# An earlier gather of softmax sums, and two attention stages written out without their loop

## The reference

```python
def _attn(x, ctx, wq, wk, wv, wo, bo, heads):
    q = (x @ wq).reshape(b, n, heads, dh).transpose(0, 2, 1, 3)      # dh = 8, heads = 20
    k = (ctx @ wk).reshape(b, j, heads, dh).transpose(0, 2, 1, 3)
    v = (ctx @ wv).reshape(b, j, heads, dh).transpose(0, 2, 1, 3)
    a = softmax(einsum('bhid,bhjd->bhij', q, k) * dh ** -0.5)
    out = einsum('bhij,bhjd->bhid', a, v)
    return out.transpose(0, 2, 1, 3).reshape(b, n, heads * dh) @ wo + bo
h1 = _ln(x, n1_g, n1_b); x = _attn(h1, h1, ...) + x
h2 = _ln(x, n2_g, n2_b); x = _attn(h2, context, ...) + x
```

## Time and profile before

| | us |
|---|---|
| median of three runs | 4166.11 |
| lowest and highest run | 4163.22, 4181.46 |
| the profiled execution's own time | 4149.92 |
| its span, from first to last instruction | 4148.1 |

### The profile page before, as it was taken

How to read it: one execution, slowest core, us unless ns; L and a number is a source line. 1 busy time by engine, 2 the same in 40 slices (tenths; PEclk the granted TensorE clock), 3 DMA queues, 4 the chain that set the end, 5 groups by cost and what they waited for, 6 DMA issues and landing times. The chain is left out here.

```text
span 4148.1 us, 103517 instructions
## 1 busy us (share of the span) xinstructions
PE 3903.9 (94%) x38592; PEld 3363.6 (81%) x38592; DVE 2324.7 (56%) x4208; ACT 2173.5 (52%) x5452; POOL 1215.8 (29%) x1313
## 2 busy tenths in 40 slices
PE   5989879999998988999999999969999999999899
PEld 3766657777777987898888888858888888888799
DVE  3666634444434555666666666645556565555554
ACT  3665635555543445555555555535555555555344
POOL 4112111111104433333333333322222222232443
PEclk7888955555558999999999999989999999999999
DMA  3322212122111000000000000000000000000000
GB/s 99 90 75 71 76 46 69 47 57 56 53 37 30 0 19 23 1 0 0 0 0 0 0 0 0 1 23 3 2 2 2 2 2 2 2 2 1 16 19 21
DMA packets 97848, 98.23 MB, mean 24 GB/s; under 512 B 27664, under 2 KB 73104, under 8 KB 97680
## 3 DMA queue, kind: packets, MB, share of 16 engines
q1 hardware_dynamic: 94480, 94.50, 8.4%
q10 hardware_dynamic: 3200, 1.31, 0.1%
HBM read 20.76 MB, written 5.24 MB: 6 GB/s over the span
## 5 line engine op out<-in xcount | busy, mean ns | idle before, releaser
L1075 POOL TENSOR_TENSOR a_probs<-a_probs,a_rsums 128x1024 f32<-128x1024 f32 x160 | 303.7, 1898 | 750.4 <-DVE a_rsums L1173 750.4
L1095 ACT ACTIVATE a_probs<-a_scores_banks,a_negmax 128x128 f32<-128x128 f32 x1280 | 367.3, 377 | 297.4 <-DVE a_negmax L1161 297.4
L1075 POOL TENSOR_TENSOR c_probs<-c_probs,c_rsums 128x616 f32<-128x616 f32 x160 | 201.5, 1259 | 768.6 <-DVE c_rsums L1173 768.5
L1095 ACT ACTIVATE c_probs<-c_scores_banks,c_negmax 128x77 f32<-128x77 f32 x1280 | 313.2, 335 | 204.5 <-DVE c_negmax L1161 204.5
L1154 DVE COPY c_outT<-c_out_bank 128x512 f32<-128x512 f32 x160 | 110.7, 692 | 369.6 <-PE c_out_bank L1315 309.2
L1438 ACT ACTIVATE f_gate<-f_up_bank,bias 128x256 f32<-128x256 f32 x320 | 151.2, 473 | 286.4 <-PE f_up_bank L323 286.4
L1462 DVE SCALAR_TENSOR_TENSOR f_hidden<-f_up_bank,bias,f_gate 128x256 f32<-128x256 f32 x320 | 149.6, 481 | 254.3 <-ACT f_gate L1438 136.2
L1154 DVE COPY a_outT<-a_out_bank 128x512 f32<-128x512 f32 x160 | 110.7, 692 | 298.6 <-PE a_out_bank L1315 246.6
L686 ACT ACTIVATE c_probs<-c_scoresT_banks 77x1024 f32<-77x1024 f32 x160 | 163.1, 1019 | 175.3 <-PE c_scoresT_banks L805 175.2
L1161 DVE TENSOR_REDUCE a_negmax<-a_scores_banks 128x4 f32<-128x512 f32 x320 | 206.2, 686 | 73.8 <-PE a_scores_banks L1216 73.8
L743 DVE TENSOR_REDUCE a_negmax<-a_scores_banks 128x8 f32<-128x1024 f32 x160 | 194.8, 1218 | 90.3 <-PE a_scores_banks L788 89.1
(11 more groups left out here) (340 smaller groups left out, 11912.9 us busy)
## 6 DMA issues: line engine op xcount, KB each, us to landing
a_q_stack<-a_q_compact SPq DMA_DIRECT2D x96, 160.0 KB
a_k_stack<-a_k_compact SPq DMA_DIRECT2D x96, 160.0 KB
c_q_stack<-c_q_compact SPq DMA_DIRECT2D x96, 160.0 KB, 3.1
c_k_stack<-c_k_compact SPq DMA_DIRECT2D x96, 96.2 KB, 2.8
x_tokens<-in_x SPq DMA_DIRECT2D x16, 320.0 KB, 5.3
a_out<-a_heads SPq DMA_DIRECT2D x64, 80.0 KB, 2.6
c_out<-c_heads SPq DMA_DIRECT2D x64, 80.0 KB, 2.0
out_x<-x_tokens SPq DMA_DIRECT2D x32, 160.0 KB, 1.9
```

The costliest lines, as they stand in the source:

```text
L1075: nc.gpsimd.tensor_tensor(probs[i][:], probs[i][:], rsums[(k - 1) % 2][:].unsqueeze(2).broadcast_to([P, UNIT, NK]), ALU.mult).then_inc(s_p ...
L1095: done = nc.scalar.activation(probs[i][:, h, :], scores[:, h // GROUP, h % GROUP * NK:(h % GROUP + 1) * NK], ACT.Exp, bias=negmax[k % 2][: ...
```

## The change

Three edits, all in `attention_small`, so both `a0` and `c0` get them. First, `run` has no loop: quads 4 to 13 are written out as straight code like the others, and every wait there compares against a constant. Second, SP issues the gather of the sums ahead of the six stack DMAs of half 1, not behind them. Third, DVE takes the reciprocal at step 9, not at step 8.

```diff
         def run(engine, step, prepare=lambda k: None):
 
-            for k in range(-2 * QUNITS, 4 * QUNITS):
+            for k in range(-2 * QUNITS, (QUADS + 2) * QUNITS):
                 step(0, k)
                 if k < 0:
                     prepare(k + 2 * QUNITS)
-            with engine.Fori(2, QUADS // 2 - 1) as q:
-                for k in range(2 * QUNITS):
-                    step(q, k)
-            for k in range(4 * QUNITS):
-                step(QUADS // 2 - 1, k)
...
+                if s == 6 and live(prev, QUADS):
+                    sp.wait_ge(s_heads, GROUPS * (prev + 1))
+                    sp.dma_start(sums[:], heads[(local - 1) % 2][1:P:32, :, :]).then_inc(s_sums_in, 16)
                 if s in (5, 6) and live(nxt, QUADS):
                     half, par = s - 5, (local + 1) % 2
...
-                if s == 6 and live(prev, QUADS):
-                    sp.wait_ge(s_heads, GROUPS * (prev + 1))
-                    sp.dma_start(sums[:], heads[(local - 1) % 2][1:P:32, :, :]).then_inc(s_sums_in, 16)
...
-                if s == 8 and live(quad_of(q, k) - 1, QUADS):
+                if s == 9 and live(quad_of(q, k) - 1, QUADS):
                     dve.wait_ge(s_sums_in, 16 * quad_of(q, k))
                     nc.vector.reciprocal(sums[:], sums[:]).then_inc(s_rsums, 1)
```

## The result

The changed kernel takes 4063.35 us in the median of 4 runs (4055.39 to 4069.51). The kernel before took 4164.66 beside it (4159.23 to 4181.46). The ratio is 0.9744, with a 95% interval of 0.9716 to 0.9772. (The plain quotient of the two medians is 0.9757, which would give 4064.9, just inside; it lies in the interval too.) Either way the kernel is faster by 20 us or more than the 4086 that were forecast. The profiled execution went from 4149.9 to 4059.68 us, by 90.2.

A forecast was written before the change was run, and what follows sets the result against it. It took `a0` as bound by a PE pause each quad and the slow clock behind it, `c0` by PE at half clock. -72.7 - 4 + 0 = -76.7 us gave 4089 on the median, forecast 4086, range 4060 to 4128.

The forecast's parts named there:

- the pauses and the clock: In `a0`, removing PE's pause each quad also removes the slow clock behind it: 72.7 us, branch stops included.
- the end of `a0`: The quad from 528.90 us, slow throughout, gets partly faster: 4 us, bounds 0 and 8.5.
- The gather and the reciprocal: In `a0`, gather issued four us earlier behind six DMAs, reciprocal at step 9: DVE's 45.9 us wait goes.
- The pushed stacks and the `out` transfers: Half 1's stacks issue 0.61 us later, `out` as before; both still land in time, so costed at nothing.
- The twelve periods: Twelve quad periods of `a0` go from 380.8 to 308.0 us: 72.7 us gained.
- The clean quad: One `a0` quad between pauses at clock 1.00, 25.67 us, taken as what every quad would take.
- `c0`: Stage at 1.2 GHz with PE always busy: no change, 0 us, bounds -13 and +7.
- The loop's branch: In `a0`, PE's four stops for want of an instruction, 4.4 us, go with straight code; included in 72.7.
- Straight code in `c0` gives nothing: Writing out `c0`'s loop gains nothing: quads took 39.50 us before the loop and 39.41 inside it.
- The fetches: Rival: 27 further instruction fetches in `c0` each stop PE 1.1 us, 30 us more, 4116 us; chance 0.04.
- The 16 us of the median: Median runs 16 us above the profiled execution, place unknown; if part was slow clock in `a0`, it goes too.
- The rival of a settled slow clock: `a0` stays at the slow clock as `c0` does: 92 us more, 4258 us; chance 0.04.

The follow-up runs named there:

- e3: Changed kernel with the reciprocal back at step 8 (straight code and early gather kept): 4061.3 us, ratio 0.9779 to the kernel before.
- e7: Changed kernel with the loop back on DVE, ACT, POOL and SP in both stages, only PE straight: 4065.7 us, ratio 0.9747 to the kernel before.
- e8: Changed kernel with the loop back on PE alone in both stages, other engines straight: 4110.7 us, ratio 0.987 to the kernel before.
- e1: Changed kernel with the hardware loops back on all engines, gather and reciprocal still moved: 4109.1 us, ratio 0.9905 to the kernel before.
- e6: Changed kernel with the hardware loop back in `c0` alone, `a0` straight: 4078.8 us, ratio 0.9782 to the kernel before.
- e10: Changed kernel with the four projection tiles of each `c0` quad computed twice: 3956.8 us, ratio 0.9509 to the kernel before.
- e9: Changed kernel with `c0` projection tiles computed twice and `c0` scores widened from 78 to 128 columns: 3925.9 us, ratio 0.9428 to the kernel before.
- e2: Changed kernel with gather and reciprocal back in their old places, straight code kept: 4143.0 us, ratio 0.9963 to the kernel before.

## Why the prediction was wrong

The mechanism of the pauses and the clock was right and the sum too small: 76.7 us forecast in the profiled execution, 90.2 measured. The step that failed is the end of `a0`, costed at 4 us because "the clock may fall anyway"; it did not fall there, and the part measured 13.6. A smaller part of the miss is chance: 6.3 us are a stretch of fast clock in `c0`.

- **The gather and the reciprocal.** As forecast: issued behind six DMAs, and no wait of DVE. The pushed stacks and the `out` transfers cost nothing; PE waits 0.5 us for maxima and DVE never for the DMAs of `out` between 145 and 450 us. That the reciprocal had to be moved too was assumed, and e3 shows that it did not.
- **The twelve periods.** 76.8 us measured, 72.7 forecast. Both contain a thirteenth pause, which the prediction took for part of a period: from restart to restart PE's twelve periods are 378.2 us, not 380.8. The clean quad was taken as 25.67 us and is 25.33 in the mean of twelve (304.00/12). The quad it was read from was still in the loop: the loops of the other engines were forecast at nothing and cost 0.2 us a quad (e7 against the changed kernel), PE's own loop nothing in a quad without a branch (e8, 25.4 us). The rest of the 0.34 is in part the last of the twelve, which takes 24.6 us.
- **The end of `a0`**, and the part ahead of the periods. Forecast 4 us, bounds 0 and 8.5; measured 11.3 + 2.3. This is the term that failed most. The quad of 29.5 us at 0.50 was expected to stay slow in part, since PE is less packed in it. In the changed kernel the clock stayed at 1.00 all through it, and it takes 21.9 us from reciprocal to reciprocal (457.61 to 479.51), where it took 31.6 with its pause: nearly the whole of the upper bound came. The last interval behind it, which the forecast left out, went from 24.3 to 20.6 us, in part because the reciprocal stands a step later.
- **`c0`.** Forecast 0, bounds -13 and +7; measured -9.5. 6.3 of it are one more stretch of fast clock (a first quad of 32.7 us, not 39.0), which is luck in the sense of the prediction: it allowed for it and could not foresee it. 3.1 are the later reciprocal and no gain. So the 0 was right: e3, with one such stretch and the reciprocal at step 8, has 559.2 us beside 558.6.
- **The loop's branch.** The step "4.4 us at the loop's branch; straight code has none of them" put the wrong price on the wrong rows. The 4.4 us were the second stop of each branch turn. The first, 2.4 to 3.2 us, lay under the DMA pause and showed as a wait for maxima. The price of the four branches with their slow clock is about 36 us (e1). The sum was not hurt, since pause and branch went together and the clean quad had neither. A forecast for the moves alone, made with the same prices, would have been wrong: it would have given e1 almost all of the gain, and e1 got less than half of it. The straight code alone was given 4 to 10 us and got 15.
- **Straight code in `c0` gives nothing.** Right for the place in which the loop lay before, and only for it: in e6 the loop costs 15 us. In the profiled execution of e8 its stops cost `c0` nothing, since the clock rose behind three of them.
- **The fetches.** The rival asked 1.1 us for each further one. They came (25 in 300 us against 3 in e1) and cost nothing: in the quads of either stage, PE's matmuls in straight code never waited for an instruction. In these runs PE stands where it branches back and the loop is fetched again, not where it runs on.
- **The 16 us of the median** that no row showed. The forecast let 3 of them go. By medians the gain is 101 us, 11 more than in the profiled executions, so about 8 us of the miss lie here. Runs of the kernel before spread from 4143 to 4204 over all comparisons and those of the changed one from 4055 to 4070, so what varied has gone with the pauses; that it was slow clock in `a0` is argued and not shown.
- **The rival of a settled slow clock** did not come: with the pauses gone the clock stood at 1.00 from 150 to 460 us.

## What to carry to other kernels

Price a pause of PE by what the clock does behind it, too: here thirteen pauses of 1.6 us cost 79.9 us, about 6 each, and it was about 9 for some and little more than 1 for others. Two causes that meet in one pause must both go before the whole of it pays. A small DMA that something waits for belongs ahead of the bulk ones, and here, beside straight code, that one move was enough. Before judging a loop or straight code on PE, count the instruction transfers in the loop: if it is fetched in every round, PE may stand at each branch, and a shift of its start may cure it. Where PE is busy throughout at half clock, look at what would raise the clock before looking for work to remove.

## What was not expected of the hardware

- A loop's cost depends on where its code begins: 0, 32 and 256 entries of shift gave stops of up to 3.5 us at each branch of `a0`, 128 gave none, and the transfers fell from 41 to 9.
- Doing more work made a stage faster: the redundant tiles of e10 took `c0` from 549.1 to 448.9 us, and with the redundant columns of e9 to 419.4.
- Pauses of 1.6 us with no DMA and no branch in them brought the mean clock of `a0` from 1.00 to 0.83. Only seven of thirteen did it, and in e2 four pauses of 1.5 to 2.0 us did not.
- A stop can be followed by a rise: in `c0` of e8 the clock went from 0.50 to 1.00 behind three of four stops of 2.9 to 3.0 us.
